# Two blocks of TensorE work moved within the part of a hand-ordered transformer kernel

## The reference

```python
xn = _ln(h, ln1_w[l], ln1_b[l])                      # first normalization
q, k, v = sh(xn @ Wq.T + bq), sh(xn @ Wk.T + bk), sh(xn @ Wv.T + bv)   # 16 heads of 8
rel = einsum('bhqd,ld->bhql', q + u, pos_emb(S))
scores = (q k^T + rel_shift(rel)) * HEAD_DIM ** -0.5
scores = where(later, NEG, scores)                    # causal
h = h + (softmax(scores) @ v) @ Wo.T + bo
fn = _ln(h, ln2_w[l], ln2_b[l])                      # second normalization
h = h + gelu(fn @ W1[l].T + b1[l]) @ W2[l].T + b2[l] # 128 -> 512 -> 128
```

## Time and profile before

| | us |
|---|---|
| median of 3 runs | 2341.55 (2340.26 to 2346.5) |
| profiled execution | 2338.84 |
| its span, first to last instruction | 2336.9 |
| TensorE busy | 2210.9 (95%) |
| VectorE busy | 1900.6 (81%) |
| ScalarE busy | 1844.3 (79%) |
| GpSimd busy | 1232.8 (53%) |

### The profile page before, as it was taken

One profiled execution on the slowest core, in us unless ns is written; L12 is line 12 of the kernel. 1 busy time (PEld: TensorE's weight loads), 2 busy tenths in 40 slices (PEclk: granted clock), 3 DMA queues, 4 the chain that ended last, 5 costly groups with the idle time before them and its releaser, 6 DMA issues. The chain is left out here.

```text
span 2336.9 us, 81563 instructions
## 1 busy us (share of the span) xinstructions
PE 2210.9 (95%) x30592; PEld 1898.1 (81%) x30592; DVE 1900.6 (81%) x4687; ACT 1844.3 (79%) x2741; POOL 1232.8 (53%) x2217
## 2 busy tenths in 40 slices
PE   5899999999999999999999999999999999799998
PEld 4788888888888888888888888888888888688887
DVE  6788888888888888888888888888878887577774
ACT  2688888888888888888888888888878888755654
POOL 4555565655555555555555555555555554433332
PEclk8899999999999999999999999999999999999999
DMA  5444434333344333334333333433343333111100
GB/s 139 119 119 130 130 110 111 107 109 105 106 110 115 107 109 105 108 108 110 108 110 107 109 108 110 111 104 107 108 120 107 108 106 92 32 28 28 28 24 19
DMA packets 268388, 229.55 MB, mean 98 GB/s; under 512 B 37216, under 2 KB 266720, under 8 KB 268000
## 3 DMA queue, kind: packets, MB, share of 16 engines
q1 hardware_dynamic: 268000, 224.32, 34.9%
HBM read 14.46 MB, written 4.19 MB: 8 GB/s over the span
## 5 line engine op out<-in xcount | busy, mean ns | idle before, releaser
L985 DVE TENSOR_REDUCE rowmax<-bank 128x4 f32<-128x1024 f32 (+1 forms) x768 | 915.5, 1219 | 172.0 <-PE bank L582 170.2
L802 ACT ACTIVATE probs<-bank 128x1024 f32<-128x1024 f32 x768 | 735.9, 1020 | 108.8 <-PE bank L641 108.7
L641 PE MATMUL bank<-qstack,kstack 64*128 64x128 f32 (+1 forms) x4096 | 426.6, 301 | 10.3 <-DMA qstack<-maxrows 10.3
L582 PE MATMUL bank<-kstack,qstack 62*128 62x256 f32 (+1 forms) x4096 | 418.5, 301 | 7.3 <-DMA qstack<-base_turned 7.3
L604 PE MATMUL bank<-maskT_half,pick_half 64*128 64x128 bf16 (+1 forms) x3072 | 270.4, 242 | 69.2 <-ACT probs L802 59.9
L641 PEld LDWEIGHTS bank<-qstack,kstack 64*128 64x128 f32 x4096 | 318.6, 193 | 11.8 <-DMA qstack<-maxrows 11.6
L582 PEld LDWEIGHTS bank<-kstack,qstack 62*128 62x128 f32 x4096 | 317.5, 193 | 7.9 <-issue 7.6
L1148 POOL CAST xn1T_parts<-xn1T 128x256 fp32r<-128x256 f32 x128 | 50.9, 397 | 456.4 <-ACT xn1T L810 456.4
L714 PE MATMUL bank<-w,hidden 128*128 128x128 f32 x2048 | 284.5, 282 | 3.5 <-ACT hidden L850 3.1
L661 PE MATMUL bank<-probs,v_pad 128*32 128x256 f32 x4096 | 271.0, 382 | 0.6 <-DVE v_tok L966 0.6
L544 PE MATMUL bank<-mask_half,pick_half 64*128 64x128 bf16 (+1 forms) x3072 | 269.3, 243 | 1.7 <-ACT xn1T L810 0.7
(11 more groups left out here) (149 smaller groups left out, 5095.3 us busy)
## 6 DMA issues: line engine op xcount, KB each, us to landing
qstack<-base SPq DMA_DIRECT2D x384, 128.0 KB, 2.5
kstack<-base SPq DMA_DIRECT2D x384, 128.0 KB, 2.5
qstack<-base_turned SPq DMA_DIRECT2D x384, 128.0 KB, 2.4
turn_x<-turn_c SPq DMA_DIRECT2D x512, 32.0 KB, 1.8
ctx_den<-ctxT_raw SPq DMA_DIRECT2D x256, 64.0 KB, 2.0
ctx_num<-ctxT_raw SPq DMA_DIRECT2D x256, 64.0 KB, 2.0
qstack<-maxrows SPq DMA_DIRECT2D x256, 16.0 KB
out<-ot SPq DMA_DIRECT2D x16, 256.0 KB, 2.4
```

What stands on the lines that cost most here:

```text
L582: last = pe.matmul(bank[:, b0 + b, i * wide:(i + 1) * wide], qstack[rows, r, p0 + i, t * 128:(t + 1) * 128], kstack[rows, r, p0 + i, 0:wid ...
L641: last = pe.matmul(bank[:, b0 + b, i * wide:(i + 1) * wide], kstack[rows, r, p0 + i, kt * 128:(kt + 1) * 128], qstack[rows, r, p0 + i, q0: ...
L802: act.activation(probs[:, k], bank[:, A_BANK[k]:A_BANK[k] + 2, :], ACT.Exp, scale=SCALE).then_inc(exp_done[k], 1)
L985: dve.tensor_reduce(rowmax[:, n % 2, t, :, p0:p0 + heads], bank[:, M_BANK[k]:M_BANK[k] + 2, :].rearrange("p b (h c) -> p b h c", h=heads), ...
```

## The change

Three edits, all in the hand-written orders. On TensorE f2 and values come ahead of M4 instead of behind it, and b4 comes ahead of down 1 instead of behind it. On VectorE the row maxima of M3 are taken ahead of those of M4, and `v_out`, which stood between them, comes behind both. No instruction is added or removed, and no wait's condition is changed.

```diff
@@ TensorE, the slot @@
                     m_masks(s - 2, 3)
                 if live(s - 2):
                     m_scores(s - 2, 3)
+                if live(s):
+                    f2(s)
+                if live(s):
+                    values(s)
                 if live(s - 2):
                     m_masks(s - 2, 4)
                 if live(s - 2):
                     m_scores(s - 2, 4)
-                if live(s):
-                    f2(s)
-                if live(s):
-                    values(s)
                 if live(s - 6):
                     up(s - 6, 1)
...
                 if live(s - 2):
                     m1(s - 2)
+                if live(s - 5):
+                    b4(s - 5)
                 if live(s - 6):
                     down(s - 6, 1)
-                if live(s - 5):
-                    b4(s - 5)
@@ VectorE, the slot @@
                 if live(s - 2):
                     max_round(s - 2, 1)
                 if live(s - 2):
+                    max_round(s - 2, 3)
+                if live(s - 2):
                     max_round(s - 2, 4)
                 if live(s):
                     v_out(s)
-                if live(s - 2):
-                    max_round(s - 2, 3)
```

## The result

The changed kernel takes 2392.59 us (median of 4 runs, 2390.24 to 2395.53) against 2340.91 us for the kernel before (median of 4, 2335.52 to 2346.5). The ratio is 1.0221, 95% interval 1.0194 to 1.0248: 52 us slower, where 62 were forecast. The profiled execution took 2390.24 us, 51.4 more than the one before.

A forecast was written before the change was run, and what follows sets the result against it. TensorE, 95% busy, waits 0.45 us at A2; after the change f2 waits for VectorE's chain. Cycle terms 3.50, 11.22, 0.43, 0.19, 0.22, 0.11, 0.03 give 15.70 against 15.19 us; 0.51 x 121 = 62 us, 2403 us, range 2380 to 2425.

The forecast's parts named there:

- `resid_2` to f2: VectorE's chain from `resid_2` to the end of M1's maxima, 3.38 us, plus 0.12 to TensorE: 3.50 us.
- the wait at f2: TensorE at L126: a new wait for M1's row maxima, some 0.6 us, 120 times, 75 us in all.
- the wait at A2: TensorE at A2's masks: the 0.45 us wait for A1's exponential goes, but the gain does not reach the end.
- From f2 to the next `resid_2`: Rest of the slot's cycle: 11.22 us as before, plus M4, height changes, b4 and the slips.
- b4's slip: TensorE, b4 ahead of down 1: its load waits for `xn2`, 0.11 us late, bounds 0 and 0.2.
- Changes of height and M4: TensorE, f2 to `resid_2`: M4 now inside this stretch, 0.43 us, and added half/full height changes, 0.19 us.
- b3's slip: TensorE at b3: waits for M4's maxima, 0.03 us late, at worst 0.15.
- the first rival: f2 is not held; TensorE's own stream sets the slot at 14.93 us, 31 us faster, 2310 us; 4%.
- The rule on height: TensorE around M4: a tiling-mode change drains the array, against putting M4 there; rows agree in direction, the page gives no price.
- The rival in which changes of height cost nothing: Cycle right, but height changes and slips cost nothing: 0.18 us a slot, 22 us, 2363 us; 8%.
- More is late: pv waits for `v_out`, or b3 and height changes reach upper bounds: 0.3 us more a slot, 2440 us; 10%.
- the waits at L680 and L661: TensorE: a wait at either line would show the prediction wrong in its sizes.

The follow-up runs named there:

- the same two edits: `stats_1` behind M1's maxima, or one extra `bn_stats` in the chain: changed kernel 2369.91 and 2416.89 us; kernel before 2341.71 and 2341.51 us.
- the last run: Kernel before with b4 ahead of down 1 and `stats_1` behind M1's maxima on VectorE, the fastest of all: 2294.63 us, ratio 0.9808.
- b4 alone: Kernel before with only b4 moved ahead of down 1; f2, values and VectorE's order as before: 2312.55 us, ratio 0.9894.
- f2 alone: Changed kernel with b4 back behind down 1; f2 and values ahead of M4 and VectorE's edit kept: 2394.57 us, ratio 1.0228 to the kernel before.
- f2, M4, values: Changed kernel with b4 back behind down 1 and values back behind M4, f2 still ahead of it: 2372.12 us, ratio 1.0147 to the kernel before.

## Why the prediction was right

**The chain.** The main steps held. `resid_2` to f2 took 3.49 us (forecast 3.50), the wait at f2 0.65 (0.6), and the wait at A2 went without reaching the end. The slot is 15.63 us (15.70). Made shorter or longer, the chain moved the time of the changed kernel; in the kernel before, the same two edits moved nothing. This shows that f2 waits for VectorE, and not for something that ends at the same time.

**The sizes.** From f2 to the next `resid_2` the forecast had 12.20 us; 12.14 were measured (1008.29 to 1004.80 + 15.63). The total came near in part because an error of 0.11 us one way met one of 0.05 the other way. By terms:

- b4's slip, forecast 0.11 us, was 0. The pair starts 0.22 us behind m1 (1003.20, 1003.42), and down 1 another 0.22 behind. The term came from the 0.12 us that a load needed after a row-maximum reduction; here `xn2` ended at 1003.30, b4's load stood at 1003.35 (row below), 0.03 us later than down 1's load in that place before, and b4 was on time at 1003.42. This is the mis-sized term: 0.11 x 121 = 13 us, more than the 10 us by which the forecast was high.
- Changes of height and M4, forecast 0.43 + 0.19 = 0.62, were 0.67: f2 to up takes 1.82 us (1008.29 to 1010.11) against 1.17 before, and up 1.53 against 1.51. Entering half height behind values costs 0.17 us (L533 takes 0.53 to the masks, 0.36 before), not the 0.09 seen at b4 to A1. f2 itself, which now begins after a wait, took 0.78 instead of 0.81 and made up for some of it.
- b3's slip, forecast 0.03, was 0.03: from b3 to pv it is 0.57 us (1011.64 to 1012.21) instead of 0.54.

```profile
1003.35 0.22 PEld L688 LDWEIGHTS bank<-eye_t,xn 128*128 128x128 f32 x2
```

One size was wrong without reaching the sum: the forecast had the wait at A2 "worth 0.45 us a slot at most" and TensorE there at 1010.61. It was worth 0.58 (see the last run), so f2 was held longer than its row says: it starts 1.22 us behind M3's masks (1007.07 to 1008.29), where M4's masks to f2 took 0.50 before, 0.72 us more. The slot did not depend on it, because the sum went around the cycle through f2 and not along TensorE's stream. The price of the first rival, 14.93 us, did, and was 0.13 us too high.

**Where the loss comes from.** The two moves are not additive: b4 alone gives 24 us back, f2 alone costs 53 (its ratio on 2341), together 52. With b4 ahead, the A2 wait and the late values go, and in their place stands the wait at f2. Without any wait the changed order could not go below 14.61 + 0.29 = 14.90 us a slot, an estimate from the rows above, and then it would still be slower than the fastest version by some 20 us (0.17 x 121); the other 0.73 us of its slot is the chain.

**The rule on height.** The forecast weighed the Trainium skill, "TensorEngine Tiling (Array Packing)" (Key Properties), that a change of tiling mode drains the array. The gaps above and the 35 us of the run f2, M4, values agree with it in direction; no run shows that a drain is the cause. The 0.35 us estimated from the Trainium skill, "TensorE: Matmul & The Clock Gate" (Single matmul latency), for the two changes was too high; 0.29 was measured, between it and the 0.19 from the rows.

**The rivals.** "f2 is not held" is false for the changed kernel. In the run with f2 alone f2 is indeed not held, but there A2 holds TensorE back instead. The rival in which changes of height cost nothing is refuted by the run f2, M4, values. "More is late" is false in size: the waits at L680 and L661 that the forecast named as a sign are there, but in the whole span TensorE waited only 2.6 us at b3 (three times) and 1.7 us at pv (once).

## What to carry to other kernels

When a wait on the critical engine is removed by moving work, look for the second chain and its slack before moving anything else: here f2 had 0.47 us to spare behind a wait that was worth 0.58, and two moves that each looked at a different wait used the same slack from both ends. Keep blocks of one array height together; in this kernel a full-height block between two half-height ones cost 0.29 us, and has to take away more waiting than that. Read slack and waits between starts of instructions, not from the idle time of a row, and look for late loads as well: at A2, at f2, at values and on VectorE, waits of about 0.1 us were hidden behind a modelled end. And where a slot comes out as expected, check its parts: two of these hidden waits made the 14.73 us look like a confirmation.

## What the runs showed of the hardware

- Leaving half-height products costs 0.07 us at the last of them (M4 takes 0.50 and M3 0.43) and 0.11 at the first full-height one (0.23 instead of 0.116), both the earlier trace rows. Entering costs 0.09 us behind fp32 transposes (b4 to A1), and 0.09 behind fp32r products (f2's last to M4's masks, 1016.07 to 1016.28 in the run f2, M4, values, where f2's products follow each other by 0.12), but 0.17 behind the fp32 value projection (changed kernel).
- A load of weights that waited for a VectorE result started 0.12 us after the end of a row-maximum reduction, and 0.05 us after the end of a `tensor_scalar` (1003.30 to 1003.35, b4's load in the changed kernel). The first was taken for the second in the forecast.
- Where a value projection's load came 0.13 us late (f2 alone), the products were stretched, from 0.53 to 0.62 us up to the next block, and the profile showed no idle time.
- In the run with b4 alone, TensorE's granted clock fell to half for 3.4 us behind a wait of 2.08 us. A late transfer thus cost its slot 3.7 us.
